# A vision tower on one core: head inverse roots spread over rows by DMA, weight and bias of q and k on ScalarE, gate logits as columns of the value projection, a new order

## The reference

```python
h = tokens(x)                                  # real part of a 16x16 FFT per patch, projected to 192
h = h + attn1(layernorm(h))                    # 12 heads of 16, softmax over the queries
h = h + attn2(layernorm(h))                    # 12 heads of 64, see below

# attn2 on x = layernorm(h)
q, k, v = split(x @ qkv_w + qkv_b)             # 12 heads of 64
q = layernorm_per_head(q) * q_norm_w + q_norm_b
k = layernorm_per_head(k) * k_norm_w + k_norm_b
a = softmax(q @ k.T / 8)                       # per head
o = a @ v
gates = from softmax(x @ wg1_w), softmax(x @ wg0_w), top 2 of softmax(x @ wg_w)   # 2, 2 and 10 logits
out = (gates per head * o) @ proj_w + proj_b
```

## Time and profile before

| | |
|---|---|
| Time, median of three | 5536.64 us |
| Profiled execution, span | 5532.4 us |
| PE busy / weight loads | 5344.4 us (97%) / 4563.7 us (82%) |
| DVE busy | 4923.8 us (89%) |
| ACT busy | 4327.1 us (78%) |
| POOL busy | 2985.7 us (54%) |
| DMA queues, share of 16 engines | 6.2% |
| Granted TensorE clock | 0.997 of 2.4 GHz |

### The profile page before, as it was taken

How to read it: one execution, slowest core, us unless ns; L and a number is a source line. 1 busy time by engine, 2 the same in 40 slices (tenths; PEclk the granted TensorE clock), 3 DMA queues, 4 the chain that set the end, 5 groups by cost and what they waited for, 6 DMA issues and landing times.

```text
span 5532.4 us, 202492 instructions
## 1 busy us (share of the span) xinstructions
PE 5344.4 (97%) x63024; PEld 4563.7 (82%) x63024; DVE 4923.8 (89%) x16193; ACT 4327.1 (78%) x17409; POOL 2985.7 (54%) x3206
## 2 busy tenths in 40 slices
...
GB/s 72 18 22 18 17 21 17 18 17 21 18 17 21 17 18 17 21 18 17 21 18 17 20 18 18 17 21 18 17 21 17 18 17 21 18 17 21 18 17 6
...
## 3 DMA queue, kind: packets, MB, share of 16 engines
...
...
## 4 chain that ended last, share of the span: by engine, by line
PE 94%; DVE 4%; issue 1%; ACT 0%; POOL 0%; SPq 0%; DVEq 0%; DMA 0%; POOLq 0%; ACTq 0%
PE bank L491 82%; PE bank L672 10%; PE bank L529 2%; DVE qk L898 1%; DVE qkn L996 1%; SPq L403 0%; ACT p L733 0%; DMA bp<-in_bp 0%; ACT pq L771 0%; POOL pq L475 0%; DVEq L902 0%; DVEq L1025 0%; DVE wqk_mean L804 0%; DVEq L992 0%; DVE nmax L903 0%
## 5 line engine op out<-in xcount | busy, mean ns | idle before, releaser
L475 POOL TENSOR_TENSOR pq<-pq,gn 99x788 f32<-99x788 f32 x768 | 1153.3, 1502 | 914.0 <-DVE gn L1011 913.9
L771 ACT ACTIVATE pq<-bank,nmax 99x197 f32<-99x197 f32 x3072 | 1300.1, 453 | 291.6 <-DVE nmax L1002 291.6
L733 ACT ACTIVATE p<-bank,nmax 99x197 f32<-99x197 f32 x3072 | 1323.1, 467 | 112.0 <-DVE nmax L903 97.3
L484 POOL TENSOR_TENSOR qkb<-qkn,ln_b 128x396 f32<-128x396 f32 x768 | 639.5, 847 | 1164.0 <-DVE qkn L996 1151.4
L777 ACT ACTIVATE pT<-bank 99x394 f32<-99x394 f32 x1536 | 767.6, 518 | 259.4 <-PE bank L672 256.4
L903 DVE TENSOR_REDUCE nmax<-bank 99x2 f32<-99x394 f32 x1536 | 843.2, 563 | 113.9 <-PE bank L491 101.7
L1002 DVE TENSOR_REDUCE nmax<-bank 99x2 f32<-99x394 f32 x1536 | 827.2, 559 | 25.7 <-PE bank L491 10.7
L733 ACT ACTIVATION_READ_ACCUMULATOR p<-bank,nmax 99x1 f32 x3072 | 762.6, 248 | 0.0
L491 PE MATMUL bank<-x2T,wqkc 128*128 128x198 f16 (+1 forms) x7680 | 752.5, 248 | 1.0 <-ACT p L733 0.7
L672 PE MATMUL bank<-ident,pq 99*99 99x99 f32 (+1 forms) x6144 | 725.3, 253 | 7.7 <-ACT pq L771 5.2
L771 ACT ACTIVATION_READ_ACCUMULATOR pq<-bank,nmax 99x1 f32 x3072 | 720.7, 235 | 0.0
...
## 6 DMA issues: line engine op xcount, KB each, us to landing
xa<-in_xa SPq DMA_DIRECT2D x128, 300.1 KB
xb<-in_xb SPq DMA_DIRECT2D x128, 300.1 KB
out_tokens<-res SPq DMA_DIRECT2D x128, 74.2 KB
out_tokens<-res SPq DMA_DIRECT2D x128, 73.5 KB
...
```

Of the source, the lines that this page charges most:

```text
L475: nc.gpsimd.tensor_tensor(pair, pair, factor, op=ALU.mult).then_inc(s_sc.up(), 1)
L484: nc.gpsimd.tensor_tensor(qkb[:, t], qkn[:, t % QKN_SLOTS], ln_b[:].unsqueeze(2).to_broadcast([128, 2, TP]), op=ALU.add).then_inc(s_qk.up( ...
L733: last = nc.scalar.activation(p1[0:TC, h, c, :], psum("s1", h)[0:TC, c * T:c * T + T], ACT.Exp, bias=nmax1[:, c, h:h + 1], accum_out=sum1[ ...
L771: last = nc.scalar.activation(pq[0:TC, h % SLOTS, c, 0:T], psum("s2", h)[0:TC, c * T:c * T + T], ACT.Exp, bias=nmax2[:, h, c:c + 1], accum ...
```

## The change

Five edits are made together.

1. `rstd` goes from PE, with `sel_rstd`, `rs_hl` and `rs_mask`. DVE now writes the refined root as fp32 in `rs` (one instruction instead of three). SP writes `rs` to a scratch tensor in HBM (`rsw`: 128 rows of 198, 101 KB), waits until that has landed, and reads it back (`rsb`: six DMAs of 64 x 4 x 198, 203 KB each), so that each head's row lands on all 64 rows of the head in `rsb`.
2. POOL `mul` multiplies `qkc` with `rsb` into `qkn` (in place of `bias`). ACT `aff` applies weight and bias: two activations 128x198 from `qkn` to `qkb`, with scale and bias taken per row from `ln_w` and `ln_b` (12 per image). `mul` number 3 and later wait for the `aff` three before, whose slot of `qkn` they take.
3. `gl` goes from PE. The 14 gate columns are appended to the value weights; `v2` number 1 and 3 have 398 columns instead of 384, and the gate steps read the logits from `v2` in SBUF.
4. The layer norms use the aggregate instruction of DVE instead of six small ones.
5. All four orders are new, SP has one too, and the pipeline is four passes deep instead of three. Two waits come with it (`h1b` for `wo` of the image before, ACT's `v1` for the scaled v of the image before).

```diff
 ORDER "pe" (a part)
-3:tok@1 0:pT_6@5 1:rstd0@0 0:pT_7@4 0:pT_8@2 1:rstd1@6 0:pT_9@5 0:pT_10@3 0:pT_11@2 0:o2_2@7 0:o2_3@3 0:o2_4@0
+2:qk0@1 2:qk1@0 3:s1_8@25 3:s1_10@34 1:s2_4@67 4:tok@1 2:qk2@0 1:pT_0@7 2:qk3@6 2:qk4@2 2:qk5@1 1:pT_1@0 1:pT_2@3
 ORDER "pool" (a part)
-3:root1 1:bias2 3:h1b 1:h2c 2:h2b 1:sc0 1:sc1 1:bias3 2:sq0 1:sc2 2:sq1 1:bias4 1:bias5 2:sq2 2:sq3 2:sq4 1:sc3 2:sq5
+1:mul0 1:mul1 1:mul2 1:mul3 3:h1b 2:sq0 1:sc0 1:mul4 2:sq1 1:sc1 4:root1 2:sq2 1:mul5 1:h2c 2:sq3 1:sc2 2:sq4 2:sq5
+    "sp": """
+4:load 1:rsb0 0:store 2:rsw0
+            def root_out(img, _):
+                sp.wait_ge(*s_rs.at(img, 1))
+                sp.dma_start(root_rows, rs[:]).then_inc(s_rsw.up(16), 16)
+            def root_in(img, _):
+                by_head = root_rows.rearrange("(u c j) n -> j c u n", u=4, c=16, j=2)
+                sp.wait_ge(*s_rsw.at(img, 16))
+                for n in range(3):
+                    for j in range(2):
+                        sp.dma_start(rsb[64 * j:64 * j + 64, 2 * n:2 * n + 2].rearrange("p t s n -> p (t s) n"),
+                                     by_head[j, n].unsqueeze(0).to_broadcast([64, 4, TP])).then_inc(s_rsb[n].up(16), 16)
-            def bias(img, t):
-                pool.wait_ge(*read_out(img, "rstd", t))
-                nc.gpsimd.tensor_tensor(qkb[:, t], qkn[:, t % QKN_SLOTS], ln_b[:].unsqueeze(2).to_broadcast([128, 2, TP]), op=ALU.add).then_inc(s_qk.up(), 1)
+            def times_rstd(img, t):
+                pool.wait_ge(*s_rsb[t // 2].at(img, 32))
+                if t >= QKN_SLOTS:
+                    pool.wait_ge(*s_qk.at(img, t + 1 - QKN_SLOTS))
+                elif not isinstance(img, int) or img > 0:
+                    pool.wait_ge(*s_qk.at(img - 1, t + 7 - QKN_SLOTS))
+                nc.gpsimd.tensor_tensor(qkn[:, t % QKN_SLOTS], qkc[:, t], rsb[:, t], op=ALU.mult).then_inc(s_qn.up(), 1)
-                    last = mm5(o[0:TC, c * NG:c * NG + NG], lambda k, r: wgate[r, k, :], lambda k, r: x2T[r, k, c, :], False)
-                last = mm5(o[0:TC, 0:384], lambda k, r: wv2[r, k, 384 * a:384 * a + 384], lambda k, r: x2T[r, k, c, :], False)
+                cols = 384 + a * NG
+                last = mm5(o[0:TC, 0:cols], lambda k, r: wv2[r, k, 384 * a:384 * a + cols], lambda k, r: x2T[r, k, c, :], False)
-                for s in range(2):
-                    last = mm(o[:, s * TP:s * TP + TP], sel_rstd[:, 2 * t + s, :], rs_hl[:])
+            def affine(img, t):
+                act.wait_ge(*s_qn.at(img, t + 1))
+                if not isinstance(img, int) or img > 0:
+                    act.wait_ge(*made(img - 1, "s2", 2 * t + 1))
+                for s in range(2):
+                    last = nc.scalar.activation(qkb[:, t, s, :], qkn[:, t % QKN_SLOTS, s, :], ACT.Identity, bias=ln_b[:, s:s + 1],
+                                                scale=ln_w[:, s:s + 1])
+                last.then_inc(s_qk.up(), 1)
-                    step(V.scalar_tensor_tensor(rootsq[:], lnvar[:], -3.0, root[:], ALU.add, ALU.mult), img, "var", 1)
-                    step(V.tensor_scalar(rs_mask[:], rootsq[:], low_rows[:, 0:1], None, ALU.mult), img, "var", 2)
-                    V.scalar_tensor_tensor(rs_hl[:], rootsq[:], -0.5, rs_mask[:], ALU.mult, ALU.subtract).then_inc(s_rs.up(), 1)
+                    dve.wait_ge(*s_rsw.at(img, 0))
+                    V.scalar_tensor_tensor(rs[:], lnvar[:], -3.0, root[:], ALU.add, ALU.mult).then_inc(s_rs.up(), 1)
-            def rstd_(img, t):
-                dve.wait_ge(*made(img, "rstd", t))
-                for s in range(2):
-                    last = V.scalar_tensor_tensor(qkn[:, t % QKN_SLOTS, s, :], psum("rstd", t)[:, s * TP:s * TP + TP], ln_w[:, s:s + 1],
-                                                  qkc[:, t, s, :], ALU.mult, ALU.mult)
```

More of the change, by code:

```diff
@@ L82, in shape_constants @@
     sel_var = np.zeros((128, H, 32), np.float32)
-    sel_rstd = np.zeros((128, H, 128), np.float16)
     for u in range(H):
         for j in range(2):
[L86 to L93, removed]
+            sel_var[64 * j:64 * j + 64, u, 2 * (u // 4) + j] = 1.0 / E2
+    c["sel_var"] = sel_var
     bias = np.ones((128, 1), np.float32)
@@ L181, in bank_uses, with build_vit_block @@
     return uses, in_bank
[L184 removed]
+def build_vit_block(nc, ins, out, root_rows, images):
     with ExitStack() as ctx:
@@ L261, in build_vit_block @@
         h1b = sb("h1b", [TC, 2, D])
-        stats, both, apart, mean, vare, rstd = ([sb(f"{name}{layer}", [TC, 2, *dims]) for layer in (1, 2)] for name, dims in
-                                                (("stats", (6,)), ("both", (2,)), ("apart", ()), ("mean", ()), ("vare", ()), ("rstd", ())))
+        stats, both, vare, rstd = ([sb(f"{name}{layer}", [TC, 2, *dims]) for layer in (1, 2)] for name, dims in
+                                                (("stats", (6,)), ("both", (2,)), ("vare", ()), ("rstd", ())))
         x1 = sb("x1", [TC, 2, D])
@@ L359, in build_vit_block @@
         s_rs = signal("head_rstd_ready", 1)
+        s_rsw = signal("head_rstd_in_rows", 16)
+        s_rsb = [signal(f"head_rstd_spread{n}", 32) for n in range(3)]
+        s_qn = signal("qk_times_rstd", 6)
         s_root = signal("head_root_steps", 3)
```

120 lines of the change are left out of this document (52 added, 68 removed).

## The result

The changed kernel takes 6315.4 us (median of four runs, 6311.2 to 6334.2) against 5536.8 before: a ratio of 1.141 (95% interval 1.140 to 1.143). It is slower by 14%; 5362 was forecast, with 0.85 on faster. The profiled execution has a span of 6309.3 us.

The account below looks back on a forecast made before the run. PE was taken to bound the kernel, a pass being its work plus 0.55 us of waiting. Start and ends 84.0 + 268, 123 passes of 40.7 and 4.2 around the span gave 5362 us; 8-in-10 range 5265 to 5490.

Parts of the forecast that it names:

- the sum: Work and waits added per engine: a pass of 42.00 - 1.48 + 0.2 = 40.7 us.
- the rivals: Four other outcomes: last gaps covered (0.14), ACT bounds (0.16), HBM trip late (0.12), no difference (0.03).
- trip late: Rival, chance 0.12: slow HBM reads of the roots, 3.7 us more a pass at half the store's rate, 5828 us.
- 0.75: PE's waits left per pass, in us, in place of 0.55: the trip's 0.2, and hand-overs through ACT.
- The trip fits, just: Roots through HBM, `ms2` to first `s2`: 12.0 us needed and available; 1 us spare to 0.4 late.
- ACT: Twelve `aff` at 0.44 us add 5.3 us a pass: from 33.76 to 39.1 us (37.1 to 40.1).
- `mul` like a square, 848 ns: POOL's product of two tensors takes 848 ns and replaces the bias, 847 ns: zero.
- DVE at 33 us: Without twelve products (4.3 us) and two root steps (0.8 us) DVE falls from 38.08 to about 33 us a pass.
- PE sheds 1.48 us: Per pass on PE: `rstd` 1.02 us and `gl` 0.53 us go, wider matmuls add at most 0.07.
- Norms, zero: On DVE the norms' new instructions replace six small ones in a list with slack: zero.
- The ends: Partial passes before and after the steady loop: 9 us shed by seven passes, and -5 us for the deeper pipeline.

Follow-up runs that it names:

- e16: e13 with `rs` computed from PSUM, `h2c` behind `sc3`, `sc0` ahead of `sq0`, a shorter pause at `nx2`, POOL's own wait behind each `mul`: 5436.8 us.
- e1: Changed kernel with one wait more: behind `root1` POOL waits until DVE's `nx1` of that image is done: 5963.8 us.
- e8: e1 with POOL's list reordered: `mul4`, `mul5` and `h2c` earlier, `sc2` directly behind the pause: 5936.3 us.
- e10: e8 with POOL's pause extended until DVE's `vs` products are done, and DVE's `ctx2` directly behind `ctx1`: 5703.8 us.
- e17: Changed kernel in which POOL waits for its own end behind each `sq` and each `mul`, nothing else: 5823.9 us.
- e13: e10 with an image's load issued behind the store, a pass earlier, and POOL also pausing behind `root2` until `nx2` is done: 5610.1 us.
- e14: e13 without the roots' way through HBM; `mul` waits for `rs` itself, the root's value in q and k left out: 5612.7 us.
- e3: Changed kernel without the twelve `aff` activations; POOL's `mul` writes `qkb` itself, weight and bias of q and k left out: 6266.6 us.
- e11: Kernel before with one part of the change alone, the layer norms using DVE's aggregate instruction: 5531.4 us.

## Why the prediction was wrong, point by point

- *"POOL: `mul` reads two tensors like the squares, 848 ns, and replaces the bias, 847 ns: zero." and "That is not on the path, but DVE's maxima will come earlier"*: here the working failed. Each engine's list was summed by itself, with durations from a trace in which POOL's runs and the normalising did not meet. Before, the bias behind `root1` waited for a DVE product (such waits are 1151.4 us in all), and POOL was idle while both normalising pairs ran. The change took that bias away, and the new list sets four squares, a product, `h2c` and `sc2` in its place, none of which waits there. They start directly behind `root1`, which is also what `nx1` waits for: they meet in every pass. The trace before has a sign of it that the sum passed over: `vs` took 209 ns at least and 695 at most, two of them 0.82 us together beside a `sq` of POOL. None of the rivals had this; "trip late" was the only one on the slower side. The sum had no term for the clock either.
- *How much*: in the pass shown the miss is 48.37 - 40.7 = 7.7 us. PE stood idle for 6.25 us where 0.75 was forecast; 3.75 of that is the wait behind the held pair. It was busy for 42.12 us where the sum gave 39.97; about 1.5 of these 2.15 us go with the clock, since the same 473 records take 40.61 us in e16 (clock 1.00, here 0.96). By the runs: e1, e8 and e10 together take 612 of the 953 us by which the forecast missed (352 + 27 + 233), and then neither `nx1` nor `vs` is held; the hold on `vs` came only with the pause and the new list. e17 takes 491 with the waits alone. e16's 138 us come from three edits at once and are not told apart.
- *The trip fits, just*: right in kind. `rs` is written 3.0 us behind `ms2` (2.7 forecast), the write takes 1.8 us, as said, and the first product starts 11.4 us behind `ms2` (10.2 forecast). PE's wait was 0.61 and 1.43 us in two passes where 0.2 was forecast, 111.8 us in the whole run. The reads stood behind the load; what the load's place alone costs is not told apart (e13), and e14 shows that nothing of the trip has to remain. The late-trip rival's 3.7 us did not come.
- *ACT*: right. 38.83 us a pass (39.1 forecast); two `aff` take 0.90 us from start to start (3008.61 to 3009.51), 0.45 each. The estimate by the Trainium skill, ScalarE: Activation LUTs (What ACT_TABLE_LOAD costs), was 444 ns; the trace agrees. Their rows last 0.60 us, not 0.50 to 0.56. They bound little (49 us in e3).
- *`mul` like a square, 848 ns*: mis-sized. Two different tensors take 1.02 us and more (mean 1138 in the changed kernel), one tensor with itself 0.85.
- *DVE at 33 us*: right once nothing is held, 32.89 in e16.
- *PE sheds 1.48 us*: too much. e16 has 41.19 - 0.28 = 40.91 us a pass without waits; the sum gave 42.00 - 0.55 - 1.48 = 39.97. `rs_hl` and `wgate` are gone; which of the other rows grew by 0.94 us is open. Less the 0.47 us by which e16's wait is under the forecast 0.75, that is 0.47 us a pass, or 59 of the 75 us that separate e16 (5437) from 5362.
- *Norms, zero*: right (e11).
- *The ends*: not tested apart.

The Trainium skill, SBUF — State Buffer (Who interferes with whom), has the rule that bears on this: copies, casts and `tensor_scalar` (the normalising instruction is one) can take DVE's second port, which is POOL's too, and two SBUF inputs take it beside a POOL instruction that reads SBUF; whoever comes second waits for the other's whole instruction. The runs agree in what is held and in what isn't (a PSUM operand: 0.35 us). They differ in how long: beside 128 rows DVE waited not for one instruction but for up to six (4.83 us).

Left open: in mixed runs DVE got in behind different counts (four POOL instructions, then two, in the changed kernel), and I have no rule for those; nor why 128x96 held nothing for long. That a shared port is what holds DVE is the page's account; the runs show the hold and its conditions.
